# Differential attention with a routed feed-forward: one exponential over a pair of PSUM banks

## The reference

```python
q, k, v = x @ Wq, x @ Wk, x @ Wv        # 32 q heads and 16 k heads of 4, 8 v heads of 8
q, k = apply_rope(q), apply_rope(k)     # each of 16 heads has two halves (q1, q2), (k1, k2)
attn1 = causal_attn(q1, k1, vcat, HD ** -0.5)
attn2 = causal_attn(q2, k2, vcat, HD ** -0.5)
attn = attn1 - lambda_full * attn2
attn = attn / rms(attn) * rms_w * (1 - LAMBDA_INIT)
x = layernorm(x + attn @ Wo)
# top-1 of 8 experts: silu(x @ w1a[e]) * (x @ w1b[e]) @ w2[e], times its probability
x = layernorm(x + ffn(x))
```

## Time and profile before

| | |
|---|---|
| median of 3 runs | 800.04 us (794.2 to 801.28) |
| the profiled execution's own time | 795.09 us |
| its span | 793.3 us |
| mean granted TensorE clock | 0.892 |
| TensorE, VectorE, ScalarE, GpSimd busy | 77%, 65%, 53%, 51% of the span |

### The profile page before, as it was taken

How to read it: one execution, slowest core, us unless ns; L and a number is a source line. 1 busy time by engine, 2 the same in 40 slices (tenths; PEclk the granted TensorE clock), 3 DMA queues, 4 the chain that set the end, 5 groups by cost and what they waited for, 6 DMA issues and landing times.

```text
span 793.3 us, 18591 instructions
## 1 busy us (share of the span) xinstructions
PE 614.7 (77%) x6770; PEld 338.7 (43%) x6770; DVE 514.8 (65%) x1139; ACT 420.9 (53%) x864; POOL 404.1 (51%) x597
## 2 busy tenths in 40 slices
PE   3337979989989999989999999996320049999990
PEld 1102434434433443433453454442210039999990
DVE  6328868968977987977897999932150016666561
ACT  1002758768767786767877778785010004444440
POOL 5025225635743754745655650432607724777774
PEclk9557999999999999999999999999555569999996
DMA  2885644644743753653673664100005113655530
GB/s 107 303 275 193 214 140 147 216 140 136 240 144 104 245 171 100 219 189 94 212 227 90 211 205 122 37 18 14 0 0 193 54 48 108 211 176 197 201 122 23
DMA packets 73006, 116.01 MB, mean 146 GB/s; under 512 B 19884, under 2 KB 42796, under 8 KB 72716
## 3 DMA queue, kind: packets, MB, share of 16 engines
q1 hardware_dynamic: 63872, 88.60, 34.9%
q0 software_dynamic: 5808, 23.24, 8.6%
q10 hardware_dynamic: 3240, 3.04, 1.1%
HBM read 71.16 MB, written 46.74 MB: 149 GB/s over the span
## 4 chain that ended last, share of the span: by engine, by line
PE 59%; POOL 13%; DVE 11%; issue 9%; ACT 3%; DMA 2%; SPq 2%; POOLq 0%; ACTq 0%; DVEq 0%
PE bank L580 14%; PE bank L695 10%; PE bank L706 5%; DVE mr L1128 5%; POOL xr L862 4%; POOL x_sorted L1015 4%; PE bank L492 3%; PE bank L510 3%; PE bank L537 3%; PE bank L501 3%; PE bank L588 2%; PE bank L519 2%; PE bank L528 2%; PE bank L591 2%; ACT work L740 2%
## 5 line engine op out<-in xcount | busy, mean ns | idle before, releaser
L1128 DVE TENSOR_REDUCE mr<-bank 128x8 f32<-128x512 f32 x576 | 358.9, 685 | 96.1 <-PE bank L510 77.5
L740 ACT ACTIVATE work<-bank 128x512 f32<-128x512 f32 x576 | 310.5, 600 | 74.4 <-PE bank L537 54.5
L580 PE MATMUL bank<-work,v_aug 128*32 128x512 f32 (+7 forms) x2048 | 172.2, 421 | 0.0
L510 PE MATMUL bank<-kd,qz 64*128 64x384 bf16 (+7 forms) x512 | 142.5, 292 | 0.0
L501 PE MATMUL bank<-kd,qz 64*128 64x128 bf16 (+7 forms) x512 | 141.6, 294 | 0.0
L537 PE MATMUL bank<-qd,kz 64*128 64x384 bf16 (+7 forms) x512 | 138.0, 285 | 0.0
L528 PE MATMUL bank<-qd,kz 64*128 64x128 bf16 (+7 forms) x512 | 134.7, 283 | 0.0
L492 PE MATMUL bank<-bits 64*128 64x128 bf16 x448 | 100.0, 226 | 6.9 <-DVE mr L1128 5.0
L519 PE MATMUL bank<-bits 64*128 64x128 bf16 x448 | 98.4, 224 | 5.7 <-ACT work L740 5.3
L838 ACT ACTIVATE work<-bank 128x256 f32<-128x256 f32 x92 | 34.8, 383 | 127.1 <-PE bank L695 115.7
L492 PEld LDWEIGHTS bank<-bits 64*128 64x128 bf16 x448 | 41.8, 94 | 120.6 <-DVE mr L1128 96.9
(11 more groups left out here) (140 smaller groups left out, 1011.2 us busy)
## 6 DMA issues: line engine op xcount, KB each, us to landing
qk_apart<-apart SPq DMA_DIRECT2D x96, 256.0 KB, 3.0
qz<-qk_apart SPq DMA_DIRECT2D x64, 192.0 KB
kz<-qk_apart SPq DMA_DIRECT2D x64, 192.0 KB
qk_parts<-parts SPq DMA_DIRECT2D x90, 128.0 KB, 2.7
qd<-qk_parts SPq DMA_DIRECT2D x64, 96.0 KB
kd<-qk_parts SPq DMA_DIRECT2D x62, 96.0 KB
xt_s<-in_xT SPq DMA_DIRECT2D x8, 512.0 KB, 4.5
x_sorted<-in_c_pad SPq DMA_DIRECT2D x1, 2990.0 KB, 12.5
```

Source lines behind the costliest of these rows:

```text
L510: pe.matmul(bk[:, wa:T], qz[lo:lo + L, kv, i - 1].rearrange("p j l -> p (j l)"), kd[lo:lo + L, kv, 0:T - wa], start=False, stop=True, skip ...
L580: m = pe.matmul(pv_b[32 * t:32 * t + 32, L * kb:T], v_aug[:, vb, kv + v, kb, :], cols, start=kb == 0, stop=True, skip_group_check=True)
L740: nc.scalar.activation(prob[:, pos, r, :], st_b[no % ST_RING][:, :], ACT.Exp, scale=HD ** -0.5).then_inc(s_sfree, 1)
L1128: V.tensor_reduce(mr[:, s % 2, u % 2, i, i:i + NB], nat_b[no % NAT_RING][:, :].rearrange("p (n t) -> p n t", t=L), AX.X, ALU.max)\
```

## The change

The natural ring has three banks instead of four. The transposed ring has two tiles of two banks each (1024 columns) instead of three single banks. The two units of a position take the two halves of one tile (the unit with the odd number the first half); any other use of this ring takes a whole tile and writes its first half. ScalarE takes the exponential of both units in one instruction over 1024 columns, after the second unit's scores are there, and it counts as one release. TensorE waits for the tile's last use, two pairs back, before either unit. The list `banks` still names eight single banks, two of them halves of each pair, for the prologue, the routing and the experts.

```diff
-    nat_at, st_at = [], []
+    nat_at, st_at, st_pair, pair_at = [], [], [], []
...
             if 0 <= g - LAG < NS:
+                st_out += 1
                 for u in (2 * t, 2 * t + 1):
                     st["exp", g - LAG, u] = len(st_at)
-                    st_out += 1
                     st_at.append(st_out)
+                    st_pair.append(len(pair_at))
+                pair_at.append(st_out)
...
                     st_out += 2 if name == "v" else 1
                     st_at.append(st_out)
+                    st_pair.append(len(pair_at))
+                    pair_at.append(st_out)
...
-NAT_RING, ST_RING = 4, 3
+NAT_RING, ST_RING = 3, 2
...
-        banks = [bank(f"bank{i}") for i in range(8)]
-        nat_b, st_b, pv_b = banks[0:4], banks[4:7], banks[7]
+        nat_b = [bank(f"nat{i}") for i in range(NAT_RING)]
+        st_b = [bank(f"st{i}", 2 * T) for i in range(ST_RING)]
+        pv_b = bank("pv")
+        banks = nat_b + [b[:, T * h:T * h + T] for b in st_b for h in range(2)] + [pv_b]
...
         def st_wait(eng, no):
-            if no >= ST_RING:
-                eng.wait_ge(s_sfree, ST_OUT[no - ST_RING])
+            if ST_PAIR[no] >= ST_RING:
+                eng.wait_ge(s_sfree, PAIR_OUT[ST_PAIR[no] - ST_RING])
...
             def st_bank(s, u):
-                return st_b[ST_NO["exp", s, u] % ST_RING]
+                r = 1 - u % 2
+                return st_b[ST_PAIR[ST_NO["exp", s, u]] % ST_RING][:, T * r:T * r + T]
...
-                    bk, done = st_b[no % ST_RING], s_st
+                    bk, done = st_b[ST_PAIR[no] % ST_RING][:, 0:T], s_st
...
-            def exp(s, u):
-                pos, r = u // 2, 1 - u % 2
-                no = ST_NO["exp", s, u]
+            def exp(s, pos):
+
+                no = ST_NO["exp", s, 2 * pos + 1]
                 wait(act, s_st, no + 1)
...
-                nc.scalar.activation(prob[:, pos, r, :], st_b[no % ST_RING][:, :], ACT.Exp,
-                                     scale=HD ** -0.5).then_inc(s_sfree, 1)
+                nc.scalar.activation(prob[:, pos, :, :].rearrange("p r t -> p (r t)"), st_b[ST_PAIR[no] % ST_RING][:, :],
+                                     ACT.Exp, scale=HD ** -0.5).then_inc(s_sfree, 1)
...
-                bk = st_b[no % ST_RING]
+                bk = st_b[ST_PAIR[no] % ST_RING][:, 0:T]
...
-                        exp(g - LAG, 2 * t)
-                        exp(g - LAG, 2 * t + 1)
+                        exp(g - LAG, t)
```

More of the change, by code:

```diff
@@ L116, in rings @@
                     st_at.append(st_out)
-    return nat, st, nat_at, st_at
-NAT_NO, ST_NO, NAT_OUT, ST_OUT = rings()
-NAT_RING, ST_RING = 4, 3
+                    st_pair.append(len(pair_at))
+                    pair_at.append(st_out)
+    return nat, st, nat_at, st_at, st_pair, pair_at
+NAT_NO, ST_NO, NAT_OUT, ST_OUT, ST_PAIR, PAIR_OUT = rings()
+NAT_RING, ST_RING = 3, 2
 def build(nc, xT, x, wq, wv, wo, lam, rms, router_w, router_b, w12, c_rope, c_sign, c_ident, c_mask, c_tri, c_iota,
```

## The result

The changed kernel takes 821.88 us in the median (820.07 to 822.91) against 800.66 us for the kernel before: a recorded ratio of 1.0275, 95% interval 1.0233 to 1.0317 (the two medians by themselves give 1.0265). The profiled execution took 820.07 us, its span 818.2 us. The forecast was 826 (804 to 848).

A forecast was written before the change was run, and what follows sets the result against it. TensorE was taken to bound the attention stage, VectorE close behind. Losses of 48 us less 19 us hidden by data waits gave 29; 795.1 + 29 = 824, with the median put at 826 us, range 804 to 848.

The forecast's parts named there:

- the cover: TensorE's waits for SyncE's data, before the q projection and a phase's first transposed mask, hide 19 us of the loss.
- The instruction: ScalarE's merged exponential of 1024 columns takes about 1.03 us; saves some 14 us where ScalarE isn't the bound.
- Position 5: Behind turn_ot both units wait for the whole pair of position 4; value product +0.49 us, in 25 phases.
- position 3: Behind turn_max both units wait for the whole pair of position 2; value product +0.39 us, in 25 phases.
- position 7: Behind turn_attn or turn_x1 at position 6, scores wait for pair 6; +0.38 us, in 12 phases.
- Value projection: At position 2 it waits for the whole of pair 2, not its first half; +1.0 us, in 7 phases.
- The natural ring: With three banks, second units wait for earlier maxima; 13.1 us in all, including 0.25 us at position 1 in 16 phases.
- Behind wo: Where wo and its statistics precede, position 1's second unit waits for maximum 0; +0.94 us, in 6 phases.
- behind rl: Position 8's second unit waits for the first maximum of position 7; +0.35 us, in 7 phases.
- The faster one: Rival: the transposed mask's 18.0 us of waits for exponentials vanish, if a pair takes under 0.81 us; 781 us; chance 0.07.
- fall of the clock: Rival: more short TensorE stalls lower the attention's granted clock; 894 us at 0.84, 848 at 0.93; 0.10 with another rival.
- The ring of three: Rival: three natural banks cost 0.2 us at each of 288 positions; 870 us; chance 0.10 together with the clock's fall.

The follow-up runs named there:

- x_early_after: The changed kernel with SyncE issuing the load of the next sequence's x ahead of the next phase's key operands; 819.29 us, ratio 1.0241.
- pair_two_early: The changed kernel with x asked for early and two exponentials of 512 columns, each releasing its half of the pair; 794.20 us, ratio 0.9951.
- nat3: The kernel before with three natural banks instead of four, its transposed ring still three single banks; 802.76 us, ratio 1.0044.
- x_early_before: The kernel before with SyncE issuing the load of the next sequence's x ahead of the next phase's key operands; 778.72 us, ratio 0.9736.
- pair_moved: The changed kernel with turn_max moved to position 3, turn_ot to 5, turn_attn and turn_x1 to 7; 806.04 us, ratio 1.0083.
- nat3_st4: The kernel before with three natural and four single transposed banks instead of four and three; 801.64 us, ratio 1.0037.

## Why the prediction was right, step by step

The direction and the mechanism held, and the size came close: +26 us forecast, +21 measured between the medians; +29 and +25 between the profiled executions. Two things in the forecast's numbers are luck. Its text adds 4.9 us for the median to 824, which makes 829 and not 826. And the cover agrees with its sum for other reasons than the sum gives.

- **The instruction.** 1034 ns worked out, 1025 measured. ScalarE's saving is there and is worth nothing, as said. Two instructions instead of one give back 25 us of 40.6 (`x_early_after` against `pair_two_early`). The Trainium skill (Perfetto Trace Analysis, section Optimizing Scalar/DVE Operations) says that breaking up the instructions of an engine which isn't saturated but leaves bubbles on others may let work be done sooner; these runs agree, by those 25 us.
- **The late start and the whole pair.** Position 5 +0.49 forecast, +0.50 measured; position 3 +0.39 and +0.39; position 7 +0.38 and +0.38 (scores of 6 to value product of 7: 272.93 to 275.46, before 219.07 to 221.22). Value projection +1.0, measured +1.03 (1.22 us behind turn_max instead of 0.19). Position 5 of those phases +0.19 forecast, +0.27 measured.
- **The natural ring.** Position 1 was put at +0.25 us and is +0.41; it was counted in 16 phases and stands in 18. Behind wo +0.94 were forecast and it is +0.83. The +0.35 behind rl isn't there in the changed kernel: position 8 starts 3.31 us behind position 6 instead of 2.93, because 7 has stalled for its pair, and in that time VectorE has caught up. In `nat3`, where 7 doesn't stall, the phase does lose 1.21 us, which is about 0.38 more than wo's 0.83. I had added two stalls in one phase of which the first pays for the second.
- **The sum.** These errors nearly cancel: 18 x 0.41 + 6 x 0.83 = 12.4 us for the natural ring, 13.1 forecast. (The 1 us of it for the first two phases can't be told: the first turn_max comes at 64.2 to 66.4 us in the thirteen kernels that have it at position 2, and at 64.2 and 66.0 us before and after the change.) With the other terms, by the forecast's counts, the measured sizes come to 48 us again. `x_early_before` and `x_early_after` are 40.6 us apart. So no term was too high by the 7 us between the two; they fit the 7.8 us for which L522 still waits in `x_early_before`, though no run takes that wait away by itself.
- **The cover.** 19 us forecast, from the waits of the earlier trace rows: 13.0 us before the q projections and 6.3 us at L522. Measured: 40.6 - 21.2 = 19.4 us. But the early x leaves the waits of L522 where they are. What it takes away besides the q projections' waits is the lower clock. In the kernel before the granted clock is 0.50 in four stretches of 3.4 us, from 113.9, 165.1, 236.8 and 349.4 us; in `x_early_before` it is 1.00 from 100 to 500 us. In the changed kernel a phase with a value projection takes 18.50 us with such a stretch in it and 16.93 without, so four of them are some 6 us, an estimate. By the sum above more than 19 us was hidden in all (48 gross, 25 net in the profiled executions, so 23), and the lower clock was in no term of the forecast. The weakest-looking step, that SyncE's queue doesn't slide along with the phases, held: from phase 7 on the load of x is issued 13.5 us or more behind the last turn_max in the kernel before, and 10.2 to 11.8 us behind it in the changed one.
- **The rivals.** The faster one needed a pair of under 0.81 us; it is 1.03. No lasting fall of the clock: 0.98 and 1.00 in the windows, with two stretches of 3.4 us at 0.50, some 3 us in all. The ring of three doesn't hurt at every position: `nat3`'s plain phases lose 0.42 us, all of it at position 1 (1.90 us long instead of 1.49). Only where positions 2 and 4 shrink, as in `pair_moved`, does it bite at 3 and 5 too.

## What to carry to other kernels

Before two instructions become one, look at when their input is complete and who waits for the first half of their output. A merged instruction starts when the last input is there and frees everything at its end; here that cost 0.87 us in each plain phase of 14 us to save some 0.5 us of an engine that wasn't the bound. And before a price is summed up, look for waits that it can hide in: about half of this one was hidden, and the fix that was worth most (21 us) was the wait that did the hiding. An idle time before a weight load is such a wait only if the matmuls beside it stand still too; in `pair_moved` they didn't.

## What the runs showed that I hadn't expected

- A gain can turn into a wait and more. `nat3_st4` shortens the plain phase by 0.22 us and is 3 us slower than the kernel before, since the q projection's waits grow to between 2.8 and 4.7 us and the granted clock falls beside each.
- The order of one DMA issue in SyncE's list was worth 21 us, more than the sum of the six waits that it removed (13 us). With them went four short stretches at the lower clock, by the estimate above some 6 of the other 8 us; no run changes the clock alone, so their share isn't shown.
